# Expert weights stored matrix by matrix, with the down matrices loaded and split during the first feed-forward

## The reference

```python
x = x + _L0_ffn_ref(_L0_cond_ref(x, cond_2048, ...), lut, gate_idx, up_idx, down_idx)
x = x + _L1_ffn_ref(_L1_cond_ref(x, cond_2048[:, None, :], ...), Wr, br, Wg, Wu, Wd)

# _L0_ffn_ref, weights w = lut[idx], INTER = 688
h = silu(x @ gate.T) * (x @ up.T);  out = h @ down.T

# _L1_ffn_ref, E = 4 experts, D_FF = 1024
probs = softmax(x @ Wr + br);  top_w, top_idx = top_k(probs, 1)
h = silu(x @ Wg[e]) * (x @ Wu[e]);  y = h @ Wd[e];  out = y[top_idx] * top_w
```

## Time and profile before

| | us |
|---|---|
| median of 3 runs | 654.2 |
| lowest and highest of them | 653.93, 662.95 |
| the profiled execution, its own time | 651.07 |
| its span, from the first to the last instruction | 649.0 |
| first attention, about | 0 to 197 |
| first feed-forward | 197 to 297 |
| second attention | 297 to 437 |
| routing | 437 to 453 |
| experts | 453 to 640 |

### The profile page before, as it was taken

How to read it: one execution, slowest core, us unless ns; L and a number is a source line. 1 busy time by engine, 2 the same in 40 slices (tenths; PEclk the granted TensorE clock), 3 DMA queues, 4 the chain that set the end, 5 groups by cost and what they waited for, 6 DMA issues and landing times. The chain is left out here.

```text
span 649.0 us, 15220 instructions
## 1 busy us (share of the span) xinstructions
PE 561.3 (86%) x5090; PEld 339.2 (52%) x5123; DVE 393.2 (61%) x812; ACT 332.3 (51%) x622; POOL 118.9 (18%) x162
## 2 busy tenths in 40 slices
PE   3798999999989999997888888851899999999991
PEld 1344555555546665554555555531466656666661
DVE  1677989898986334554988888876134333432331
ACT  2366677777755244448888888830222221222120
POOL 3302222222602000000000000002132332233211
PEclk9999999999999999997999999985899999999997
DMA  8865555554760000006866666641111111111110
GB/s 283 220 122 150 126 126 125 124 129 112 154 160 11 0 1 1 1 1 162 201 157 155 154 160 159 157 122 17 33 36 38 48 47 30 33 49 40 36 31 3
DMA packets 29414, 60.30 MB, mean 93 GB/s; under 512 B 5989, under 2 KB 16647, under 8 KB 26952
## 3 DMA queue, kind: packets, MB, share of 16 engines
q1 hardware_dynamic: 20624, 25.68, 13.5%
q0 software_dynamic: 6432, 18.46, 13.2%
q10 hardware_dynamic: 2328, 15.75, 10.2%
HBM read 58.75 MB, written 7.81 MB: 103 GB/s over the span
## 5 line engine op out<-in xcount | busy, mean ns | idle before, releaser
L1311 DVE TENSOR_REDUCE nmax<-PB 128x2 f32<-128x512 f32 x128 | 85.6, 682 | 20.8 <-PE PB L854 19.1
L539 ACT ACTIVATE probs<-PC 128x512 f32<-128x512 f32 x128 | 73.9, 609 | 20.4 <-PE PC L866 19.4
L783 ACT CAST probs<-PC 128x1024 bf16<-128x1024 f32 x19 | 19.2, 1012 | 113.6 <-PE PC L1222 113.6
L1747 DVE TENSOR_TENSOR probs<-PC,probs 128x1024 bf16<-128x1024 f32 x19 | 23.3, 1225 | 80.9 <-ACT probs L783 80.9
L1214 PE MATMUL PA<-arena,probs 128*128 x227 | 54.4, 391 | 7.6 <-issue 3.9
L854 PE MATMUL PB<-small 64*128 64x256 bf16 x256 | 51.1, 291 | 6.6 <-DVE nmax L1311 6.5
L1233 PE MATMUL PD<-arena,probs 128*128 x456 | 52.9, 273 | 2.5 <-issue 2.5
L1214 PE MATMUL PB<-arena,probs 128*128 x210 | 48.6, 379 | 0.9
L1233 PEld LDWEIGHTS PD<-arena,probs 128*128 128x128 bf16 x456 | 44.2, 98 | 8.3 <-issue 3.2
L454 POOL DMA_DIRECT2D arena<-in_w_all x16 | 8.5, 532 | 206.9 <-DVE arena L1588 120.0
L866 PE MATMUL PC<-small 64*128 64x256 bf16 x256 | 45.8, 281 | 0.5 <-DVE small L1327 0.5
(11 more groups left out here) (213 smaller groups left out, 1099.8 us busy)
## 6 DMA issues: line engine op xcount, KB each, us to landing
arena<-idx_low ACTq DMA_DIRECT2D x15, 1024.0 KB
wst<-in_w_all SPq DMA_DIRECT2D x48, 256.0 KB, 2.8
arena<-in_w_all POOLq DMA_DIRECT2D x16, 384.0 KB, 5.4
arena<-in_idx_all SPq DMA_DIRECT2D x1, 2176.0 KB, 10.2
arena<-in_cond SPq DMA_DIRECT2D x16, 128.0 KB, 7.8
small<-in_x SPq DMA_DIRECT2D x16, 128.0 KB, 10.3
arena<-idx_low POOLq DMA_DIRECT2D x2, 1024.0 KB, 15.0
tok_r<-rows SPq DMA_DIRECT2D x1, 2048.0 KB, 16.9
```

Source lines behind the costliest of these rows:

```text
L539: nc.scalar.activation(probs[:, c, o], PC[:, o], ACT.Exp, scale=SCALE0).then_inc(S["ex"], 1)
L1311: v.tensor_reduce(nmax[:, c, s, :], PB[:, s * 512:(s + 1) * 512].rearrange("p (a k) -> p a k", k=T), AX.X, ALU.max, negate=True).then_inc( ...
```

## The change

The arena is laid out as gate high, gate low, up high, up low, down high, down low. The down matrices then lie at f32 columns 16,384 to 24,576, behind everything that the first feed-forward keeps, apart from `spread` and `hot`. GpSimd loads their high halves in two loads of 4,096 columns as soon as its stores of zeros are issued and the lookups are over; SP loads the f32 values in sixteen pieces of 512 columns through `wst[:, 2]`; DVE splits them in `down_low`, one piece after a hidden tile from tile 4 of chunk 0 on (in chunk 2 at tiles 0 to 2 and 5, in chunk 3 at tiles 0 and 1 and two at tile 5). In the second attention `weight_low` is called twice a round, for gate and up, and twice in the routing.

```diff
-        w_parts = arena[:].bitcast(BF16)
-        all_hi, all_lo = w_parts[:, 0:3 * HALF], w_parts[:, 3 * HALF:6 * HALF]
...
-        PIECE = 3 * HALF // B
-        SUB = PIECE // 3
+        w_parts = arena[:].bitcast(BF16).rearrange("p (k h c) -> p k h c", k=3, h=2)
+        (wg_hi, wg_lo), (wu_hi, wu_lo), (wd_hi, wd_lo) = ([w_parts[:, k, h, :] for h in range(2)] for k in range(3))
+        SUB = HALF // B
+        by_matrix = w_all.rearrange("p (k c) -> p k c", k=3)
...
+            sp.wait_ge(S["pad"], 32)
+
+            def down_piece(q):
+                if q < 2:
+                    sp.wait_ge(S["cl"], B)
+                else:
+                    sp.wait_ge(S["wdl"], q - 1)
+                sp.dma_start(wst[:, 2, q % 2 * SUB:(q % 2 + 1) * SUB], by_matrix[:, 2, q * SUB:(q + 1) * SUB]
+                             ).then_inc(S[f"wdt{q % 2}"], 16)
+
+            for q in range(B):
+                down_piece(q)
             sp.wait_ge(S["x1"], B)
-            sp.wait_ge(S["pad"], 32)
...
             def weight_pieces(u, par):
-                for n in range(3):
+                for n in range(2):
                     if not (isinstance(u, int) and u < 2):
                         sp.wait_ge(S[f"wsl{n}"], u - 1)
-                    sp.dma_start(wst[:, n, par * SUB:(par + 1) * SUB], w_all[:, bass.ds(u * PIECE + n * SUB, SUB)]
+                    sp.dma_start(wst[:, n, par * SUB:(par + 1) * SUB], by_matrix[:, n, bass.ds(u * SUB, SUB)]
                                  ).then_inc(S[f"wst{n}{par}"], 16)
...
+            pool.wait_ge(S["lmm"], LCH)
+            for n in range(2):
+                o = slice(n * HALF // 2, (n + 1) * HALF // 2)
+                pool.dma_start(wd_hi[:, o], by_matrix[:, 2, o]).then_inc(S[f"wdh{n}"], 16)
             pool.wait_ge(S["x1"], B)
+
             def weight_high(u, par):
                 if not (isinstance(u, int) and u < 2):
-                    pool.wait_ge(S["wsl2"], u - 1)
-                o = bass.ds(u * PIECE, PIECE)
-                pool.dma_start(all_hi[:, o], w_all[:, o]).then_inc(S[f"wsh{par}"], 16)
+                    pool.wait_ge(S["wsl1"], u - 1)
+                o = bass.ds(u * SUB, SUB)
+                pool.dma_start(w_parts[:, 0:2, 0, o], by_matrix[:, 0:2, o]).then_inc(S[f"wsh{par}"], 16)
...
+            def down_low(*pieces):
+
+                for q in pieces:
+                    dve.wait_ge(S[f"wdh{2 * q // B}"], 16)
+                    dve.wait_ge(S[f"wdt{q % 2}"], 16 * (q // 2) + 16)
+                    o = slice(q * SUB, (q + 1) * SUB)
+                    v.tensor_tensor(wd_lo[:, o], wst[:, 2, q % 2 * SUB:(q % 2 + 1) * SUB], wd_hi[:, o], ALU.subtract
+                                    ).then_inc(S["wdl"], 1)
...
                 if after:
                     low_parts(i + 1)
-                if weights:
-                    weight_low(i - 1, 2, 1 - par, half)
+
+            def meanwhile0(m):
+                if m == 0:
+                    modulation()
+                if m >= 4:
+                    down_low(m - 4)
+
+            def meanwhile1(m):
+                down_low(m + 2)
 
             def meanwhile2(m):
+                if m < 3:
+                    down_low(m + 8)
...
+                if m == 5:
+                    down_low(11)
...
+                if m < 2:
+                    down_low(12 + m)
+                if m == 5:
+                    down_low(14, 15)
...
-            for n in range(3):
+            for n in range(2):
                 weight_low(LAST, n, 1, U - 1)
```

More of the change, by code:

```diff
@@ L118, in bf @@
             return v
-        w_parts = arena[:].bitcast(BF16)
-        all_hi, all_lo = w_parts[:, 0:3 * HALF], w_parts[:, 3 * HALF:6 * HALF]
-        (wg_hi, wu_hi, wd_hi), (wg_lo, wu_lo, wd_lo) = ([v[:, k * HALF:(k + 1) * HALF] for k in range(3)]
-                                                        for v in (all_hi, all_lo))
-        PIECE = 3 * HALF // B
-        SUB = PIECE // 3
+        w_parts = arena[:].bitcast(BF16).rearrange("p (k h c) -> p k h c", k=3, h=2)
+        (wg_hi, wg_lo), (wu_hi, wu_lo), (wd_hi, wd_lo) = ([w_parts[:, k, h, :] for h in range(2)] for k in range(3))
+        SUB = HALF // B
+        by_matrix = w_all.rearrange("p (k c) -> p k c", k=3)
         xall = f32(B, T).rearrange("p (b t) -> p b t", b=B)
@@ L144, in program @@
         h_lo = bf(MT, CH).rearrange("p (m t) -> p m t", m=MT)
-        assert max(at[0], at_hot) <= 3 * HALF
+        assert at_hot <= 3 * HALF and at[0] <= 2 * HALF
         def w0(w, which, kt, m):
@@ L292, in program @@
             "qT", "qTe", "kTe", "s3", "e3", "v1", "c3", "cq1", "rd3", "on", "oT", "t3", "te3", "lg",
-            "wst00", "wst10", "wst20", "wst01", "wst11", "wst21", "wsh0", "wsh1", "wsl0", "wsl1", "wsl2",
+            "wst00", "wst10", "wst01", "wst11", "wsh0", "wsh1", "wsl0", "wsl1", "wdh0", "wdh1", "wdt0", "wdt1", "wdl",
             "rv", "r", "rx", "rp", "te", "slot", "rows", "asel", "bsel", "inv", "tokn",
@@ L1191, in _ @@
             ins.then_inc(S["inv"], 1)
-            for n in range(3):
+            for n in range(2):
                 pe.wait_ge(S[f"wsl{n}"], B)
+            pe.wait_ge(S["wdl"], B)
             pe.wait_ge(S["te"], 1)
@@ L1586, in weight_low @@
                 dve.wait_ge(S[f"wst{n}{par}"], 16 * half + 16)
-                o = bass.ds(u * PIECE + n * SUB, SUB)
-                v.tensor_tensor(all_lo[:, o], wst[:, n, par * SUB:(par + 1) * SUB], all_hi[:, o], ALU.subtract
+                o = bass.ds(u * SUB, SUB)
+                v.tensor_tensor(w_parts[:, n, 1, o], wst[:, n, par * SUB:(par + 1) * SUB], w_parts[:, n, 0, o], ALU.subtract
                                 ).then_inc(S[f"wsl{n}"], 1)
+            def down_low(*pieces):
[5 more added lines that the diff above has]
+                                    ).then_inc(S["wdl"], 1)
             def body1(i, par, half, results=True, before=True, after=True, weights=True):
@@ L1638, in meanwhile3 @@
                     low_parts(0)
-            hidden_chunk(0, lambda m: modulation() if m == 0 else None)
-            hidden_chunk(1, lambda m: None)
+                if m < 2:
+                    down_low(12 + m)
+                if m == 5:
+                    down_low(14, 15)
+            hidden_chunk(0, meanwhile0)
+            hidden_chunk(1, meanwhile1)
             hidden_chunk(2, meanwhile2)
```

## The result

The changed kernel took 651.45 us in the median of 20 runs (644.63 to 660.58), the kernel before 654.37 beside it: a ratio of 0.991 with the interval 0.988 to 0.993. Three more comparisons of the same pair gave 0.997 (0.994 to 1.000), 0.991 (0.987 to 0.996) and, from six runs, 0.987 (0.979 to 0.995). The ratios are taken over fast runs alone, those within 1.5% of a kernel's own fastest, which leaves out seven of the changed kernel's twenty runs (all from 654.46 us on) but only two of the kernel before's (from 662.93 on), so that they make the gain look larger than it is. Over all runs the medians of the four comparisons lie 2.9, 0.5, 3.3 and 0.9 us apart and the means 3.6, 0.7, 3.3 and 2.9 (two runs of the kernel before of over 1000 us left out); weighted by their spread the means give 2.7, with an interval of 1.5 to either side.

What follows compares the result with a forecast made beforehand. PE was taken to bound the first feed-forward, DVE's chain the routing, and no single one of three nearly full engines the second attention. -2.6 - 0.63 + 0 = -3.2 us took 654.2 to 651.0, range 646 to 659.

Steps and rivals of the forecast that it cites:

- Part 1: Second attention: one DVE subtraction fewer each round gains 0.20 us in 13 rounds, 2.6 us; ends 0 and 8.4.
- ACT keeps the round: Rival, second attention: ACT's order is the whole of the round, so only the routing gains: 653.6 us; chance 0.15.
- waited for in full: Rival, second attention: each round gains the removed subtraction's whole 0.60 us, giving 645.2 us; chance 0.10.
- Part 2: Routing: two subtractions instead of three on DVE's chain, 1.26 for 1.89 us, gaining 0.63; ends 0 and 0.7.
- Part 3: First feed-forward: sixteen added DVE subtractions, 10.9 us, hidden behind PE's work; costed at nothing, at most 1 us together.
- Part 4: First feed-forward: DVE's first down_low waits for GpSimd's first high load, landing at 221.0; cost starts at 221.6, so no stall.
- L: Landing time of GpSimd's first down high-half load: 210.85 + 2.1 + 6.3 + 1.7 = 221.0 us; bounds 219.3 and 227.3.
- waits there for the whole first load: First feed-forward: DVE reaches the first down_low at 218.8 and waits until GpSimd's first high load lands, 221.0.
- The late load: Rival, first feed-forward: two high loads share engines, first lands at 227.3, PE waits 5.7 us; 656.7 or 661.7; chance 0.25.
- Part 5: Second attention: GpSimd's loads shrink from 384 to 256 KB and SP's pieces from 48 to 32; gains nothing.
- The sum: Whole kernel: -2.6 - 0.63 + 0 = -3.2 us, from a median of 654.2 to 651.0; chance 0.50.
- theory B: Follow-up expectation, whole kernel: something else in the change gives as much again, 6 us in all, ratio 0.991 or less.

## Why the prediction came out right

- **Part 1, the subtraction of each round (0.20 us, 13 rounds, 2.6):** right in size and cause. 0.19 measured, 0.13 of it ahead of the exponential and 0.06 ahead of the values, as worked out; putting the instruction back restores 8.22, and taking one more away gains nothing. The ends of 0 and 0.60 are both excluded, and with them the rivals "ACT keeps the round" and "waited for in full". Reading one round instruction by instruction gave this; the busy time of the stage would have said 0.60. Two readings in it were wrong without harm. DVE does wait on the way to the next `kT_out`, 0.65 us a round for ACT (L1551), so it was not full before the change either. And `mean_squares` could not have started at 367.39, since ACT's squares (L648) ended at 367.44. Of the 13 rounds, the one with the low clock gained nothing (10.54 and 10.61 from the second `kT_out` to the third) and the next gained 0.40.
- **Part 2, the routing (0.63):** 1.89 became 1.28, 0.61 gained.
- **Part 3, sixteen subtractions at nothing:** 0.2 us at the most by the length of the first feed-forward.
- **Part 4, the first load (L = 221.0, no stall):** the end of the sum was near, 221.16 and 220.18 in two executions, and the terms were not. The high load landed 8.0 us after its issue where 2.1 + 6.3 + 1.7 = 10.1 had been summed; without the 1.7 for SP's pieces, which did not hold it up, 8.4 would have been close. SP's piece, costed at 0.85 of the engines' time and not as a thing that is waited for, landed after 9.7. The step that failed is "waits there for the whole first load". It was luck that the two errors nearly met. Counted from the issue of the high load, the first `down_low` was summed to come after 10.15 us and came after 10.7 to 11.2 in seven traces. By the earlier trace rows it may start 3.5 us behind the start of the remainder ahead of it, and 2.9 were predicted, a margin of 0.6. Measured are 3.6 in the execution shown, just over the edge, and 2.3 to 3.1 in the other six. The late load, as rival, did not occur: the high loads came one behind the other (8.0 and 13.0 us, issued about 0.6 apart), as the pair of the earlier trace rows with 128 partitions and unlike the pair at 23.1. The Trainium skill's "DMA: Bandwidth & Descriptors" (section "Anatomy of one DMA — SWDGE (gpsimd) path") would give 6.8 us for this load by an estimate; measured are 7.5 to 8.2, above it, and nearer to it than to the 10.1 of the prediction.
- **Part 5, fewer bytes at nothing:** right; with the third subtraction back and the bytes still fewer the time is that of before.
- **The sum (-3.2):** the rows account for 13 x 0.19 + 0.6 = 3.1. The medians of all runs are 2.9, 0.5, 3.3 and 0.9 us apart, the means of the four comparisons together 2.7, give or take 1.5. The ratios of 0.991 and 0.987 would stand for 6 us and more, theory B of the expectations, but over all runs the means give ratios of 0.994, 0.999, 0.995 and 0.996, and no row was found that the change made shorter beyond the 3.1. Single executions of either kernel differ by more than the gain, through spells of a low clock in both attentions and in the first feed-forward. That the changed kernel's fastest run is faster by 2 to 8 us in each comparison (644.5 to 647.1 against 649.0 to 652.5) is not explained.

## What to carry to other kernels

An instruction that leaves a full engine gains only what the next wait leaves: walk from it to the next instruction of another engine and take the smallest slack on the way (0.20 of 0.60 here), and expect the second such instruction to gain nothing once another engine holds the round. When work is moved to an idle engine and an idle stage, what decides is the first transfer; place the first wait late enough that the slowest transfer it needs has landed beside all the others in flight, and ask that of the small ones of other queues too. A wait at the head of an in-order engine is paid in full by the engine behind it from the moment that one is out of work (4.0 us of idle time and 1.7 of clock for two tiles' difference here).

## What the runs showed that was not expected

- A small transfer beside a large casting one: 256 KB on SP's queue landed after 2.6 us alone and after 9.7 and 12.5 us beside two loads of 1024 KB on GpSimd's queue, though it needs little of the engines' time. It is the small transfer that was late, not the large one, which landed after 7.5 us alone and after 7.8 to 8.2 beside the pieces.
- Fewer bytes in shorter runs save little of the engines' time. In the changed kernel's second attention ten loads of 256 KB, in two runs a partition, took this (336 to 418.6), and the kernel before's of 384 KB took that (340 to 422.6):
```profile
q0 software_dynamic: 2817, 2.71, 25.1%
```
```profile
q0 software_dynamic: 1441, 3.92, 29.9%
```
25.1% and 29.9% of 82.6 us are 2.07 and 2.47 us a load: a third fewer bytes, twice the packets, 16% less time.
- After an idle time of PE of 4.0 us the clock was down for about four microseconds; after one of 1.5 us, with PE at full work before it, for about as long, with 1.7 us lost by either; after the idle time of the earlier trace rows for ten. The price of a stall in clock is not one number, and a short stall can cost more in clock than in idle time.
